# Reading x a second time by columns, so that the query path needs no transposes of it and no normalized copy

## The reference, cut to what matters

```python
x = x + cross_attention(layernorm(x), ctx_1024)     # W_q, W_k, W_v, W_out and biases
x = x + top2_of_8_experts(layernorm(x))             # router Wr, W1, W2, silu gate

def layernorm(x, eps=1e-05):
    m, v = mean(x), var(x)
    return (x - m) / sqrt(v + eps)
```

## Time and profile before

| | |
|---|---|
| median of 3 runs | 1176.52 us (1175.81 to 1178.37) |
| the profiled execution | 1174.99 us, of which the span of its instructions is 1173.2 us |
| busy in the span | TensorE matmuls 97%, its weight loads 87%, VectorE 80%, ScalarE 66%, GpSimd 51% |
| first `scores` | 24.86 us after the span's start, the second at 30.19 us |
| a slot in the steady stretch | 7.76 us, and 7.88 us in those with q = 1 |

### The profile page before, as it was taken

How to read it: one execution, slowest core, us unless ns; L and a number is a source line. 1 busy time by engine, 2 the same in 40 slices (tenths; PEclk the granted TensorE clock), 3 DMA queues, 4 the chain that set the end, 5 groups by cost and what they waited for, 6 DMA issues and landing times. The chain is left out here.

```text
span 1173.2 us, 38427 instructions
## 1 busy us (share of the span) xinstructions
PE 1136.0 (97%) x12514; PEld 1018.2 (87%) x12515; DVE 941.5 (80%) x2949; ACT 774.8 (66%) x1635; POOL 597.5 (51%) x729
## 2 busy tenths in 40 slices
PE   6999999999999999988999999999999999999995
PEld 4677777777777777777999999999999999999995
DVE  6789999999999999898888877776776777677772
ACT  5677777777777776666766766666666666666652
POOL 6345677767766776595564333333333333333333
PEclk9999999999999999999999999999999999999998
DMA  5123333333333333536787776777777777767743
GB/s 191 36 74 94 110 106 100 113 113 104 104 109 113 111 102 105 188 127 215 191 221 201 200 212 171 217 195 190 189 210 200 172 198 210 192 172 214 194 109 68
DMA packets 106631, 180.18 MB, mean 154 GB/s; under 512 B 14400, under 2 KB 80128, under 8 KB 106368
## 3 DMA queue, kind: packets, MB, share of 16 engines
q1 hardware_dynamic: 74448, 136.54, 36.4%
q0 software_dynamic: 25584, 35.54, 16.0%
q10 hardware_dynamic: 6464, 6.36, 1.7%
HBM read 132.57 MB, written 45.29 MB: 152 GB/s over the span
## 5 line engine op out<-in xcount | busy, mean ns | idle before, releaser
L1782 POOL DMA_INDIRECT out_rows<-y_gated,block_tokens x114 | 187.2, 1642 | 257.3 <-DMA out_rows<-y_gated,block_tokens 107.4
L675 PE MATMUL bank<-block_T_hi,w_hi 128*128 128x256 f32 x912 | 261.1, 286 | 0.7 <-DVE block_T_lo L1397 0.7
L677 PE MATMUL bank<-block_T_hi,w_lo 128*128 128x256 f32 x912 | 256.1, 281 | 0.0
L676 PE MATMUL bank<-block_T_lo,w_hi 128*128 128x256 f32 x912 | 256.1, 281 | 0.0
L839 ACT ACTIVATE probs_T<-bank 128x512 f32<-128x512 f32 x256 | 132.1, 603 | 64.7 <-PE bank L512 64.7
L675 PEld LDWEIGHTS bank<-block_T_hi,w_hi 128*128 128x128 f32 x912 | 173.9, 191 | 0.9 <-DVE block_T_lo L1397 0.9
L676 PEld LDWEIGHTS bank<-block_T_lo,w_hi 128*128 128x128 f32 x912 | 173.2, 190 | 0.0
L677 PEld LDWEIGHTS bank<-block_T_hi,w_lo 128*128 128x128 f32 x912 | 172.9, 190 | 0.0
L1095 DVE TENSOR_REDUCE row_max<-bank 128x4 f32<-128x512 f32 x256 | 157.9, 675 | 13.0 <-PE bank L493 13.0
L1715 POOL DMA_INDIRECT routed_rows<-rows,dest_i x128 | 129.7, 1013 | 37.3 <-issue 33.4
L1380 DVE TENSOR_TENSOR w_lo<-w_raw,w_hi 128x1024 fp32r<-128x1024 f32 x114 | 134.1, 1218 | 6.2 <-ACT w_hi L940 6.2
(11 more groups left out here) (211 smaller groups left out, 2941.0 us busy)
## 6 DMA issues: line engine op xcount, KB each, us to landing
w_raw<-in_L_ffn_W SPq DMA_DIRECT2D x114, 512.0 KB, 4.7
half_w<-in_L_ffn_W SPq DMA_DIRECT2D x42, 512.0 KB, 5.6
block_rows<-routed_rows SPq DMA_DIRECT2D x57, 272.0 KB, 4.8
x_in<-in_x SPq DMA_DIRECT2D x64, 128.0 KB, 2.4
ctx_T<-in_ctx SPq DMA_DIRECT2D x16, 512.0 KB, 4.5
x_res<-in_x SPq DMA_DIRECT2D x64, 128.0 KB, 2.6
out_rows<-x SPq DMA_DIRECT2D x64, 128.0 KB, 2.3
w_lo<-in_L_ffn_W ACTq DMA_DIRECT2D x8, 512.0 KB, 4.4
```

The costliest lines, as they stand in the source:

```text
L675: mm(dst, w1h[k][:, c, at:at + P], xh[:, k, c, :], start=(c == 0), stop=False)
L676: mm(dst, w1h[k][:, c, at:at + P], xl[:, k, c, :], start=False, stop=False)
L677: last = mm(dst, w1l[k][:, c, at:at + P], xh[:, k, c, :], start=False, stop=(c == KC - 1))
L1782: nc.gpsimd.indirect_dma_start(out=out[:, :], out_offset=bass.IndirectOffsetOnAxis(ap=tk[:, u % U, t:t + 1], axis=0), in_=yg[:, u % 2, t, ...
```

## The change: what it does, and the diff

The host passes x a second time as `x_T`, laid out by columns like the context. A group of 4 tiles is one load of 512 KB; ScalarE copies the hi part (two instructions a group) and GpSimd subtracts for the lo part (two a group). `W_q` loses its mean at the start: TensorE averages it with a 128x128 matrix of 1/256 and VectorE subtracts. The normalized tile, its transposes and the copies from PSUM are gone. x itself is still loaded for the statistics; rstd of 4 tiles goes to a small DRAM tensor and comes back as one row of 512 numbers, repeated over the 128 partitions (`rb`). In the slots, ScalarE copies q out of PSUM, GpSimd multiplies it by `rb` in place (read at a step of 4 numbers), and one slot later ScalarE adds the bias in place. For the first group VectorE multiplies on the way out of PSUM.

```diff
+        def store_rstd(eng, g):
+            eng.wait_ge(s_rs1, 2 * (g + 1))
...
+            eng.dma_start(rr[g].rearrange("(p q) -> p q", p=P), rs1[:, g % 2, :]).then_inc(s_rst, 16)
+
+        def load_rstd(eng, g):
+            eng.wait_ge(s_rst, (g + 1) * 16)
...
+            eng.dma_start(rb[:, g % 2, :], rr[g].rearrange("(o n) -> o n", o=1).to_broadcast([P, GB * P])).then_inc(s_rld, 16)
...
             def before():
+                load_xt(0)
                 for t in range(4):
                     load_x(t)
+                load_c(0)
                 sp.dma_start(consts[:], cst).then_inc(s_const, 16)
-                load_c(0)
...
                 if t % GB == 0 and real(t + 3 * GB):
                     load_c(t // GB + 3)
+                if t % GB == 0 and real(t + 2 * GB):
+                    store_rstd(sp, t // GB + 2)
+                if t % GB == 1 and real(t + 2 * GB):
+                    load_rstd(sp, t // GB + 2)
+                if t % GB == 3 and real(t + 4 * GB):
+                    load_xt(t // GB + 4)
...
                     pv(t - 1, 1)
-                if real(t + 9):
-                    pe.wait_ge(s_xl, t + 9)
-                    to_T(t + 9, bank[6])
...
+            def q_bias(g, o):
+                act.wait_ge(s_qm, 2 * g + o + 1)
+                return nc.scalar.activation(q_at(g, o), q_at(g, o), ACT.Identity, bias=bqc[:, o:o + 1])
...
+                xT_hi(0, 0)
+                xT_hi(0, 1)
                 w_part_hi(0)
-                ln1_norm(2)
-                ln1_norm(3)
                 w_part_hi(1)
...
+                store_rstd(act, 0)
                 w_part_hi(2)
...
+                load_rstd(act, 0)
+                xT_hi(1, 0)
+                xT_hi(1, 1)
+                act.wait_ge(s_bke, 1)
+                for o in range(2, 4):
+                    k_out(0, o, bank[4 + o])
+                store_rstd(act, 1)
+                act.wait_ge(s_ones, 1)
+                for q in range(2, 4):
+                    v_rows(q, bank[4 + q])
+                for o in range(2):
+                    q_bias(0, o).then_inc(s_ev, 1)
+                for q in range(2):
+                    v_rows(q, bank[4 + q])
                 w_part_hi(3)
...
                 if real(t + 4):
                     v_rows(t + 4, bank[7])
-                if real(t + 9):
-                    xT_hi(t + 9, bank[6])
                 if q % 2 == 0 and real(GB * (g + 1)):
                     ctx_hi(g + 1, q // 2)
-                if real(t + 10):
-                    ln1_norm(t + 10)
+                if q == 3 and real(GB * (g + 2)):
+                    xT_hi(g + 2, 0)
+                if q == 1 and real(GB * (g + 1)):
+                    xT_hi(g + 1, 1)
+                if real(GB * g) and 1 <= q < 3:
+                    q_bias(g, q - 1)
...
+            def q_scaled(g, o):
+                pool.wait_ge(s_ev, GB * g + o + 1)
+                pool.wait_ge(s_rld, (g + 1) * 16)
...
+                row = row.rearrange("m (q p) -> m q p", q=GB)
+                G.tensor_tensor(row, row, rb[:, g % 2, :].rearrange("m (p q) -> m q p", q=GB), ALU.mult).then_inc(s_qm, 1)
...
+                if q % 2 == 0 and real(GB * (g + 1)):
+                    xT_lo(g + 1, q // 2)
...
-                if t % 2 == 1 and real(t + 11):
+                if q < 2 and real(GB * g):
+                    q_scaled(g, q)
+                if q == 2 and real(t + 10):
+                    rstd1(t + 10)
+                if q == 3 and real(t + 11):
                     rstd1(t + 11)
```

More of the change, by code:

```diff
@@ L451, in split3 @@
                 return last
-            def to_T(t, bk):
-                pe.wait_ge(s_xn, count(t))
-                for c in range(KC):
-                    last = nc.tensor.transpose(bk[:, c * P:(c + 1) * P], xn[:, t % LB, c * P:(c + 1) * P], ident)
-                last.then_inc(s_xT, 1)
             def qk_proj(g, o, bk):
                 par = g % 2
-                if o == 0:
-                    pe.wait_ge(s_xl, GB * (g + 1))
+                if o == 0 and g < 2:
+                    pe.wait_ge(s_xl, KC * (g + 1))
+                if o == 0 and g >= 2:
+                    pe.wait_ge(s_xlp, KC * (g - 1))
                 if o == 2:
@@ L800, in ctx_hi, with k_out, q_at, q_out @@
                 nc.scalar.activation(t_hi[:, g % 2, KC + c, :], c_in[:, g % 2, c, :], ACT.Copy).then_inc(s_chi, 1)
-            def qk_out(g, o, bk):
+            def k_out(g, o, bk):
                 par, c = g % 2, o % 2
+                act.wait_ge(s_qk, GB * g + o + 1)
+                if g >= 2:
+                    act.wait_ge(s_st, GB * (g - 1) * NCH)
+                for e in range(2):
+                    last = nc.scalar.activation(kT[:, par, c, e, :], bk[:, :], ACT.Identity,
+                                                bias=bke[:, c, e:e + 1], scale=consts[:, C_PAR + e:C_PAR + e + 1])
+                last.then_inc(s_ev, 1)
+            def q_at(g, o):
+                return qT0[:, g % 3, :] if o == 0 else qT1[:, g % 2, :]
+            def q_out(g, o, bk):
                 act.wait_ge(s_qk, GB * g + o + 1)
@@ L1213, in before @@
                 last.then_inc(s_bvr, 1)
-                for q in range(GB):
-                    xT_lo(GB + q, bank[q])
                 ln1_stats(LB + 2)
@@ L1864 @@
     full["L0_xattn_W_out"], full["L0_xattn_b_v"] = full["L0_xattn_W_out"][:, by_tile], full["L0_xattn_b_v"][by_tile]
[L1865 removed]
+    for n, by_column in (("x", "x_T"), ("ctx_1024", "ctx_1024")):
+        full[by_column] = full[n].reshape(NB // GB, GB, P, KC, P).transpose(0, 4, 3, 1, 2).reshape(NB // GB, P, KC, GB * P)
     laid = {n: _np.ascontiguousarray(full[n].T if n in _TRANSPOSED else full[n]) for n in _INS}
```

208 lines of the change are left out of this document (110 added, 98 removed).

## The result

| | before | after |
|---|---|---|
| median of 5 runs, us | 1176.52 (1175.43 to 1178.9) | 1184.56 (1183.59 to 1184.67) |
| ratio | 1 | 1.0062, 95% interval 1.0048 to 1.0077 |
| span of the profiled execution, us | 1173.2 | 1181.7 |

The account below looks back on a forecast made before the run. TensorE up to `scores_T`, then ScalarE's `exps`, were taken to pace each slot. Start +1.5 and SyncE's queue +0.7 on 1174.99 gave 1177.2; with the median 1.5 above that execution, 1178.7 us, range 1174.5 to 1184.5.

Parts of the forecast that it names:

- the slots: Steady attention slots: TensorE loses 0.57 us in each of 54, hidden behind ScalarE's `exps`, so nothing gained; slots stay 7.76 us.
- Rival 1: Slots: TensorE's work is the bound after all; up to 0.57 us less in each of 54, 1146; chance 0.07.
- all else 0: Closing sum: beyond the start, +1.5 us, and SyncE's queue, +0.7 us, nothing in the kernel changes the time.
- The start: Before the steady slots: VectorE's chain behind the late `W_out` copy puts second `scores` at 31.7 instead of 30.19.
- The term +1.5: Start of the kernel: second `scores` come 1.5 us later; with slow casts 3.8.
- The first `scores` were forecast at 24.1: Start: first `scores` at about 24.1 us instead of 24.86; coming earlier is of no use.
- The casts: Start, VectorE: two casts take 0.34 us together with GpSimd idle, upper bound 2.66; they took 1.33 each before.
- the limit of 21: Start: the first group's rstd, back from DRAM at 18 or 19 us, costs nothing up to about 21.
- SyncE's queue: Slots: three more entries a group ahead of `minus_max_rows`; 0.7 us in all, bounds nothing and 11 us.
- GpSimd's multiplication: Slots: multiplying q by rstd taken at 1.29 us, upper bound 2.6, at no cost to the total.
- Rival 3: Slots: GpSimd or SyncE's queue becomes late in every group, 1182 to 1190; chance 0.22.

Follow-up runs that it names:

- after_early_work: Changed kernel plus four unused 256-column TensorE matmuls a slot ahead of `scores_T`, slots 5 to 54: 1268.44 us, 1.0536 of the kernel before.
- after_warm: Changed kernel plus unused matmuls in idle TensorE stretches of the start: 1264.28 us, 1.0485 of the kernel before.
- after_again: Changed kernel, unedited, run again on chips 6 and 7: 1262.14 us, 1.0488 of the kernel before.
- before_new_places: Kernel before with only its tiles moved to the changed kernel's SBUF places: 1211.03 us, 1.0050 of the kernel before.
- before_64: Kernel before with 64 spare bytes ahead of `w1_raw0`: 1207.02 us, 1.0025 of the kernel before.
- before_apart: Kernel before with 64 spare bytes ahead of `w1_hi1`, setting the odd blocks' operands apart: 1193.7 us, 0.9911 of the kernel before.
- before_all_apart: Kernel before with operands of odd blocks, projections and output projection set 64 bytes apart: 1193.65 us, 0.9912 of the kernel before.
- after_old_places: Changed kernel with its tiles back at the SBUF places from before the change: 1260.71 us, 1.0456 of the kernel before.
- after_scatter_first: Changed kernel with GpSimd's scatter ahead of its lo parts of x and context: 1247.65 us, 1.0372 of the kernel before.

## Why the prediction was right or wrong

**Right: the slots.** 54 slots lost 0.57 us of TensorE's work each and stayed at 7.76 us; the third piece of `pv` waits for ScalarE in all but one of them. Rival 1 is refuted, and `after_early_work` shows that it was the place and not the amount.

**Wrong: a term is missing.** The sum ended with "all else 0", and the step that failed is that the parts of the program which the diff leaves alone were never priced. The overlay moved `w1_hi0` and `w1_lo0` to places where the matmuls of and around the even blocks are 2 to 6 ns slower, some two thousand times: +5.9 us when done alone. A turn of 23.1 us grows by 24 × 2.2 + 24 × 5.6 + 12 × 4.4 + 24 × 0.3 ns = 0.25 us, and 17.6 turns by 4.4, against 4.35 measured. No row ahead of the forecast told of such an effect; that the diff moves the buffers could be seen in it.

**The start: right in mechanism, too small in one trace.** Forecast: second `scores` at 31.7. Measured: 31.9 to 32.2 in four traces of the changed kernel's order (one of them `after_warm`) with a granted clock of 1.00 from 28 to 34 us, 33.86 in the result's. The term +1.5 was +3.67 there. The working took TensorE's pace for given. In that execution thirteen intervals between the first projections were slow, against seven in the kernel before, and the q projection of slot 0 ran at a granted clock of 0.50. The first `scores` were forecast at 24.1 and came at 26.00 (25.1 in `after_again`). The casts were cheap, as taken (0.22 us), and VectorE had rstd at 20.04, inside the limit of 21, but it did wait 0.87 us for it.

**SyncE's queue** was given 0.7 us and cost nothing in the steady slots: `minus_max_rows` is waited for in none. While W2 comes in, the wait is 2.2 us in four slots, against 1.6 before.

**GpSimd's multiplication** was taken at 1.29 us. The groups of the kernel after, 60 to 440 us, show it beside the subtraction:

```profile
L1761 POOL TENSOR_TENSOR q_T<-q_T,ln_rstd_rows 128x512 f32<-128x512 f32 x25 | 38.5, 1541 | 0.0
...
L1753 POOL TENSOR_TENSOR t_lo<-x_T,t_hi 128x512 fp32r<-128x512 f32 x24 | 30.8, 1285 | 0.0
```

A fifth more than the subtraction, and still without cost on that chip. The Trainium skill ("GPSIMD Engine Reference", section Performance pitfalls for Q7 kernels) gives half as much again for such a read; the measured 1.54 us decides.

**Rival 3** was wrong on the chip of the result: its time, 1182 to 1190, came out, but for another reason. On chips 6 and 7 a late GpSimd does reach TensorE, by way of the scatter, which the prediction did not have, and at 1 us a slot (9.37 against 8.33 in `before_new_places`) rather than 0.4 us a group.

**Together:** 8.0 us of medians, less 5.9 for the places, leaves 2.1 for everything that was forecast at 2.2. The two intervals, 5.6 to 9.1 and 4.5 to 7.6 us, are too wide for that agreement to mean much, and in the trace it is made of errors that cancel: the start lost 3.67 us and not 1.5, and the way from there to the first silu gave 0.9 back where 0.7 of loss was forecast. That the time came out near the top of the range is luck; the range was not drawn for the places.

## What to carry to other kernels

A change that allocates moves its neighbours: compare the SBUF places of the two programs, and the time of an untouched stretch in the two traces, before a cause is looked for in the edit. Work taken from the busiest engine is worth nothing if it lay in the shadow of another's wait; a slot of the kernel before that already lacks the work shows it ahead of time. And a result of one chip is one chip's: the same kernel cost 0.6% here and 4.9% there. A slower start in one trace is not yet the edit's: unedited starts of the kernel before and its variants had their second `scores` 1.4 us apart.

## What the runs showed of the hardware

- In the expert blocks the pitch (start to start) of pairs of a 128x128 weight load and a 256-column float32 matmul depends on the places of the operands in their partition. It was 118.2 to 120.0 ns in all stretches where the two operands' rests at a division by 128 were equal, and 113.3 to 117.8 ns in all where they differed by 64. Means over 16 or 17 turns in ns, "=" for equal rests and "/" for different ones:

| kernel | `up`, even block, two halves | half block's `down` | `up`, odd block, two halves | the two `down` | turn, us |
|---|---|---|---|---|---|
| before | / 117.8, 113.9 | / 113.4 | = 119.7, 119.4 | = 120.0, 119.5 | 23.10 |
| after, `before_new_places` | = 120.0, 119.5 | / 117.8 | = 120.0, 119.3 | = 120.0, 119.4 | 23.35 |
| `before_64` | = 118.5, 118.2 | / 117.8 | = 119.9, 119.4 | = 120.0, 119.5 | 23.27 |
| `before_apart` | / 117.8, 113.9 | / 113.3 | / 113.3, 114.5 | / 113.3, 117.6 | 22.61 |
| `before_all_apart` | / 113.3, 117.7 | / 117.8 | / 117.8, 115.1 | / 113.3, 114.2 | 22.67 |

  So the rest tells the two ranges apart, and not what a stretch takes within its range: the half block's `down` went from 113.4 to 117.8 though its own operands stayed where they were. In the slots the output projection gained only 0.9 ns a pair by it. It is a rule that worked in these moves, not a mechanism; what in the chip causes it stays open.
- On chips 6 and 7 the completion of `scores_T` is seen only 0.6 to 0.7 us after the end of a scatter by GpSimd that overlaps it (61 us over slots 10 to 53 in `after_again`), and in the result's traces, taken for a third chip, it is not delayed (1 us). Why the chips differ, and what couples the two, is open. Placing the scatter outside the whole slot's path was not tried.
- The granted clock from 28 to 34 us of one and the same start was 1.00 in three executions (`after_again`, `after_old_places`, `after_scatter_first`) and 0.72 in two (the result's, `after_early_work`). The way from the first maxima to the second `scores` took 3.1 us at the one and 4.1 at the other. In both cases TensorE had stood idle for up to 2 us behind the first `scores`. What decides between them is open.
